# A transformer block on one core: the five engines' calls written in a new order, without the batch loop, and with fewer unread products

## The chip, the cores and the metric

The kernel runs on one core of one Trainium2 chip. The metric is the device time of one execution in microseconds. The core's engines, by the names of the profile, are PE (TensorE, the matrix unit; its weight loads are PEld), DVE (VectorE), ACT (ScalarE), POOL (GpSimd) and SP (SyncE), which issues most of the DMAs.

## The reference, cut to what matters

The input is 8 batches of 512 rows and 256 columns. Each batch goes through one transformer block with a causal window of 128, and then through a gated feed-forward that looks at the row before.

```python
def _L0_attn_ref(x, Wq, bq, Wk, bk, Wv, bv, Wo, bo, W1, b1, W2, b2, ln1_w, ln1_b, ln2_w, ln2_b):
    B, L, D = x.shape                      # 8, 512, 256; 16 heads of 16
    band = (j > i) | (i - j > WINDOW)      # WINDOW = 128
    h = layer_norm(x, ln1_w, ln1_b)
    q = (h @ Wq + bq).reshape(B, L, N_HEADS, HEAD_DIM)   # k and v likewise
    scores = jnp.einsum('blhd,bmhd->bhlm', q, k) * scale + bias
    attn = jax.nn.softmax(scores, axis=-1)
    ctx = jnp.einsum('bhlm,bmhd->blhd', attn, v).reshape(B, L, D)
    x = x + ctx @ Wo + bo
    h2 = layer_norm(x, ln2_w, ln2_b)
    return x + jax.nn.gelu(h2 @ W1 + b1) @ W2 + b2       # W1: 256 x 1024

mod = (_silu(c) @ wmod).reshape(B, 6, 1, -1)   # sa, ca, ga, sb, cb, gb
h = _layernorm(x) * (1 + ca) + sa
x = x + ga * _L0_attn_ref(h, ...)
h = _layernorm(x) * (1 + cb) + sb
r = sigmoid((mu_r * h + (1 - mu_r) * h_prev) @ W_r.T)    # h_prev: the row before
k = (mu_k * h + (1 - mu_k) * h_prev) @ W_k.T
x = x + gb * (r * (square(relu(k)) @ W_v.T))
```

## The kernel before

The work is cut into 8 batches; u counts the 16 half-batches of attention (eight heads each) and i the 16 half-batches of rows in the feed-forward parts; gp counts the 64 groups of four heads. Every engine has its own instruction stream, written by hand as a list of calls such as `project(3)` or `scores(7, 2, 4)`. A call waits on semaphores for its inputs and for its buffers, issues its instructions, and raises a semaphore. So the order on an engine is exactly the order of its list, and an engine stands still when the call whose turn it is lacks an input, whatever is ready behind it.

One half-batch of attention goes through these calls. `transposes_a` (PE), `high_a` (ACT) and `low_a` (DVE) turn the normalised rows and split them into a high and a low half precision part. `project` (PE, 12 products) makes queries and keys, `high_qk` (ACT) and `low_qk` (DVE) split them. `maxima(u, 0..3)` on PE makes upper bounds of the scores and the call of the same name on DVE reduces them (tile nmax); the four of one u take turns on PE and DVE. `max_rows` (PE), `max_copy` (ACT), `low_m` (DVE) and `max_send` (ACT) put the maxima beside the queries. `stacks` (SP) brings queries and keys into the layout of `scores` (PE, two pieces per group: `(gp, 0, 2)` and `(gp, 2, 4)`); `exps` (ACT) takes the exponential of each piece, `select` (POOL) cuts the band, `sums` (POOL) adds for the denominators, and `context(u)` (PE) multiplies with the values, which `values` (PE) and `copy_v` (ACT) have made. `copy_den` (ACT), `fold_den`, `save_den`, `spread_den` (SP), `divide` and `scale_c` (DVE) finish the softmax. `out_project` (PE) and `residual_a` (DVE) end attention.

The first feed-forward of a half-batch i is `stats_b` (DVE), `rstd_b` (POOL), `norm_b` (ACT), `transposes_b` (PE), `high_b` (ACT), `low_b` (DVE), `up` (PE), `gelu` and `high_f` (ACT), `low_f` (DVE), `down` (PE). The second is `residual_b` (DVE), `rstd_c` (POOL), `norm_c` (ACT), `transposes_d` (PE), `modulate` (ACT), `mix` (DVE), `keys`, `receptance` and `values_b` (PE), `square` and `gate` (ACT), `gated` (DVE), `scale_o` (POOL), `output` (DVE) and `store` (SP).

All this is a pipeline over the batches. The first part of the lists (the fill) is written out and starts the batches one after the other; PE, ACT, DVE, POOL and SP then have a loop (`for b in range(3, 7)` on PE and ACT) whose body holds one batch's worth of each kind of work; the last part empties the pipeline. Between the calls of the fill PE has `warm(n, times)`: products of an identity matrix with itself whose result is never read (line 239, each shows in the trace as two matmul records). Up to the end of the fill there are 146 of them, and 16 more in `warm_end(0, 16)` (line 244) before the last `keys`. Setup work (rounding and splitting of weights, `setup_w1`, `setup_wo`, `setup_w2` on ACT; squares, gates and norms, `setup_gates` and `setup_f1` on POOL) stands in the fill too.

The lines of the trace: 239 `warm`, 244 `warm_end`, 267 to 269 `project`, 285 to 287 `values`, 303 and 307 `maxima`, 342 `scores`, 361 to 381 `context`, 398 `out_project`, 430 to 432 `up`, 486, 474 and 498 `keys`, `receptance` and `values_b` on PE; 958 to 964 `high_qk`, 976 `copy_v`, 983 `copy_den`, 997 `exps`, 1146 `setup_w1` on ACT; 1530 `maxima`, 1562 `residual_a`, 1667 `output`, 1623 `mix` on DVE; 2104 to 2112 `setup_gates`, 2174 to 2179 `select` on POOL.

## Time and profile before

| what | value |
|---|---|
| time, median of 3 runs | 622.04 us (620.81 to 622.77) |
| time of the profiled execution | not listed apart from its span; the fastest of the 3 runs is 620.81 us |
| its span in the trace | 620.5 us |
| PE busy | 567.8 us, 92% |
| ACT busy | 446.9 us, 72% |
| DVE busy | 403.2 us, 65% |
| POOL busy | 380.3 us, 61% |

The span is the time from the first to the last instruction in the trace. Busy time of PE counts the unread products as well. PE is the engine with the most work in every stretch, but its share is an average over the fill, the loop and the end, which have different limits.

### The profile page before, as it was taken

How to read it: one execution, taken by the hardware profiler on the slowest of the kernel's cores; microseconds unless marked ns; L12 is line 12 of the kernel's file. 1: busy time of each engine (PE TensorE's matmuls, PEld its weight loads, DVE VectorE, ACT ScalarE, POOL GpSimd, SP SyncE). 2: the span in 40 equal slices, each digit the busy share in tenths (PEclk: the TensorE clock that was granted, in tenths of full speed). 3: DMA queues.
4: the chain of work that ended last, by engine and by line, in shares of the span. 5: the costliest groups of instructions: out<-in, count | busy, mean ns of one | idle time of the engine just before them, and what ended most of it. 6: DMA issues, size and time to landing. Idle time of an engine off the chain costs nothing.

```text
span 620.5 us, 16499 instructions
## 1 busy us (share of the span) xinstructions
PE 567.8 (92%) x6528; PEld 444.8 (72%) x6528; DVE 403.2 (65%) x830; ACT 446.9 (72%) x745; POOL 380.3 (61%) x610
## 2 busy tenths in 40 slices
PE   5889988999898999999898989899999989999996
PEld 2668757777776777677667767677767768878785
DVE  4676746686464788576867686578867475375453
ACT  2527447499968777897879786987788798955542
POOL 4387324657937957675767678586657378943430
PEclk9989989899999999999999999999999999999999
DMA  5635423434503051351235132533134242110111
GB/s 176 246 103 133 124 77 78 112 75 116 137 18 101 25 139 52 97 143 56 69 90 153 60 87 76 146 93 89 52 80 112 70 116 52 54 46 26 34 44 35
DMA packets 46364, 55.74 MB, mean 90 GB/s; under 512 B 11643, under 2 KB 33469, under 8 KB 46286
## 3 DMA queue, kind: packets, MB, share of 16 engines
q1 hardware_dynamic: 44454, 53.81, 31.4%
q8 instruction: 52, 0.85, 0.6%
q10 hardware_dynamic: 1832, 0.87, 0.6%
q14 instruction: 26, 0.21, 0.1%
HBM read 22.31 MB, written 4.49 MB: 43 GB/s over the span
## 4 chain that ended last, share of the span: by engine, by line
PE 50%; ACT 17%; DVE 15%; issue 7%; POOL 7%; DMA 1%; SPq 1%; ACTq 1%; DVEq 0%; POOLq 0%
PE rest L486 4%; PE rest L498 4%; PE rest L447 3%; PE rest L449 3%; PE rest L448 3%; DVE nmax L1530 3%; PE quad L342 3%; ACT rest L1048 3%; PE rest L361 3%; PE rest L474 3%; PE rest L239 3%; PE quad L398 2%; ACT hid_hi L1058 2%; ACT p L997 2%; DVE hid_lo L1590 2%
## 5 line engine op out<-in xcount | busy, mean ns | idle before, releaser
L2174 POOL TENSOR_SCALAR_AFFINE_SELECT p<-p 128x448 f32<-128x448 f32 x64 | 41.5, 649 | 102.8 <-ACT p L997 80.5
L1530 DVE TENSOR_REDUCE nmax<-quad 128x8 f32<-128x1032 f32 x64 | 79.0, 1234 | 2.2
L430 PE MATMUL rest<-bt_hi,w_hi 128*128 128x256 f16 x256 | 70.2, 274 | 5.3 <-DVE hid_lo L1590 5.1
L997 ACT ACTIVATE p<-quad,scale_s 128x576 f32<-128x576 f32 (+1 forms) x77 | 62.3, 822 | 15.7 <-PE quad L342 15.4
L1048 ACT ACTIVATE rest<-rest,bias,scale_g 128x256 f32<-128x256 f32 x128 | 63.0, 532 | 11.2 <-PE rest L432 11.0
L447 PE MATMUL rest<-w_hi,hid_hi 128*128 128x256 f16 x256 | 69.9, 273 | 0.9 <-DVE hid_lo L1590 0.9
L432 PE MATMUL rest<-bt_hi,w_lo 128*128 128x256 f16 x256 | 69.8, 273 | 0.0
L431 PE MATMUL rest<-bt_lo,w_hi 128*128 128x256 f16 x256 | 69.8, 273 | 0.0
L449 PE MATMUL rest<-w_hi,hid_lo 128*128 128x256 f16 x256 | 69.8, 272 | 0.0
L448 PE MATMUL rest<-w_lo,hid_hi 128*128 128x256 f16 x256 | 69.8, 272 | 0.0
L1590 DVE SCALAR_TENSOR_TENSOR hid_lo<-rest,inv_f,hid_hi 128x512 f16<-128x512 f32 x64 | 46.8, 744 | 25.1 <-ACT hid_hi L1058 24.8
L2189 POOL TENSOR_TENSOR ps<-p 128x384 f32<-128x384 f32 x56 | 56.7, 1012 | 1.4
L2191 POOL TENSOR_TENSOR ps<-ps,p 128x320 f32<-128x320 f32 x56 | 49.1, 877 | 4.4
L342 PE MATMUL quad<-q_st,k_st 100*128 100x192 f16 (+3 forms) x468 | 45.1, 228 | 6.8 <-DVE x L1562 2.7
L1058 ACT ACTIVATE hid_hi<-rest,inv_f 128x512 f16<-128x512 f32 x64 | 43.4, 687 | 4.5 <-PE rest L449 2.2
L342 PEld LDWEIGHTS quad<-q_st,k_st 100*128 100x128 f16 x468 | 33.1, 97 | 16.7 <-issue 3.7
L1527 DVE COPY_PREDICATED quad<-later,quad 128x248 f32<-128x248 int16 x64 | 26.8, 418 | 28.2 <-PE quad L307 28.1
L361 PE MATMUL rest<-p,v_blk 128*32 128x192 f32 (+2 forms) x1024 | 41.2, 314 | 0.9 <-POOL p L2179 0.9
L361 PEld LDWEIGHTS rest<-p,v_blk 128*32 128x32 f32 x1024 | 31.9, 112 | 12.8 <-issue 5.8
L239 PE MATMUL rest<-ident 128*128 128x128 f32 x292 | 41.1, 292 | 0.0
L239 PEld LDWEIGHTS rest<-ident 128*128 128x128 f32 x292 | 37.1, 202 | 1.8 <-issue 0.7
L1517 DVE SCALAR_TENSOR_TENSOR k_two<-kc,pick,k_two 128x512 f16<-128x512 f32 x32 | 24.7, 827 | 20.1 <-ACT kc L964 20.1
(239 smaller groups left out, 1531.9 us busy)
## 6 DMA issues: line engine op xcount, KB each, us to landing
k_st<-k_two SPq DMA_DIRECT2D x64, 128.0 KB, 2.5
v_blk<-vn SPq DMA_DIRECT2D x16, 512.0 KB, 6.4
q_st<-q_two SPq DMA_DIRECT2D x64, 64.0 KB, 2.6
k_st<-k_two SPq DMA_DIRECT2D x64, 64.0 KB, 2.0
rb<-den_rows SPq DMA_DIRECT2D x16, 256.0 KB
x<-x SPq DMA_DIRECT2D x16, 256.0 KB, 3.0
out<-x SPq DMA_DIRECT2D x16, 256.0 KB, 2.2
xa<-x SPq DMA_DIRECT2D x7, 512.0 KB, 4.8
```

The costliest lines, as they stand in the source:

```text
L239: e.matmul(psum[4 if n < WARM else 7 if n < WARM + 5 else 5][:, 0:P], ident[:, :], ident[:, :], start=True, stop=True)
L342: last = e.matmul(bank[:, c0:c0 + w], k_st[0:MR, half, j, s * P:(s + 1) * P], q_st[0:MR, half, j, s * KW + q0:s * KW + q0 + w], start=True ...
L361: e.matmul(bank[32 * j:32 * j + 32, s * KW:s * KW + w], v_blk[:, s % 2, s // 2, half, 2 * j * HD:2 * (j + 1) * HD], p32[(4 * u + j) % SLOT ...
L430: e.matmul(dst, w1_hi[:, k, ms], bt_hi[:, k, :], start=(k == 0), stop=False)
L431: e.matmul(dst, w1_hi[:, k, ms], bt_lo[:, k, :], start=False, stop=False)
L432: last = e.matmul(dst, w1_lo[:, k, ms], bt_hi[:, k, :], start=False, stop=(k == KC - 1))
L447: e.matmul(dst, hid_hi[:, m, ts], w2_hi[:, m, :], start=(m == 0), stop=False)
L448: e.matmul(dst, hid_hi[:, m, ts], w2_lo[:, m, :], start=False, stop=False)
L449: last = e.matmul(dst, hid_lo[:, m, ts], w2_hi[:, m, :], start=False, stop=(m == MF - 1))
L997: e.activation(p32[gp % SLOTS][:, c0:c0 + 2 * w].rearrange("p (n c) -> p n c", n=2), (rest if gp < APART else quad)[:, b0 % HQ:b0 % HQ + 2 ...
L1048: e.activation(dst, dst, ACT.Gelu_apprx_tanh, bias=bias_1[:, m:m + 1], scale=scale_g[:, 0:1]).then_inc(s_gl, 1)
L1530: e.tensor_reduce(nmax[:, :, :, qt].rearrange("p a j -> p j a"), quad[:, :, 2 * QB - 2:2 * WIN].rearrange("p j (c a) -> p j a c", a=2), AX ...
```

## The change

The lists of all five engines are written in another order, and the loop over batches is written out, so that the order can differ from batch to batch. The calls themselves are the same ones, and each does what it did. Of the 146 unread products before the end 82 are left, in other places; the 16 of `warm_end` now stand behind the last `values_b`. A few waits are added, with which statistics and a load don't overwrite what is still to be read. `hold(e, s, n)` is the kernel's own helper, a wait that is left out where an earlier one implies it.

PE, from the start of its lists to the first batches of the fill, then the place of `values_b(0)`, the head of the loop, and the end:

```diff
+            warm(0, 2)
             setup_first()
             setup_mod()
             setup_attn()
             setup_peak()
             setup_row()
-            warm(0, 9)
+            warm(1, 5)
             transposes_a(0)
-            warm(1, 3)
+            warm(2, 14)
             project(0)
-            warm(2, 10)
             warm(3, 3)
+            warm(4, 2)
             maxima(0, 0)
+            warm(5, 11)
             maxima(0, 1)
-            warm(4, 4)
-            warm(5, 1)
-            warm(6, 1)
             maxima(0, 2)
-            warm(7, 6)
+            setup_mod_rest()
             maxima(0, 3)
-            setup_mod_rest()
             max_rows(0)
             values(0, 0)
+            project(1)
+            setup_mod_cols(0, 0)
             values(0, 1)
-            project(1)
             scores(0, 0, 2)
-            warm(8, 10)
+            setup_mod_cols(0, 1)
+            warm(9, 3)
             maxima(1, 0)
-            setup_mod_cols(0, 0)
-            warm(9, 3)
-            warm(10, 3)
             scores(0, 2, 4)
-            setup_mod_cols(0, 1)
+            setup_mod_cols(1, 0)
+            setup_mod_cols(1, 1)
+            scores(1, 0, 2)
             maxima(1, 1)
-            warm(11, 3)
-            scores(1, 0, 2)
-            warm(12, 3)
-            warm(13, 1)
+            warm(11, 2)
+            warm(12, 2)
+            warm(14, 5)
             maxima(1, 2)
             scores(1, 2, 4)
-            warm(14, 6)
             scores(2, 0, 2)
             maxima(1, 3)
-            warm(15, 4)
-            setup_mod_cols(1, 0)
-            setup_mod_cols(1, 1)
+            warm(15, 5)
+            setup_f1()
             scores(2, 2, 4)
             transposes_a(1)
+            setup_bias(0)
             scores(3, 0, 2)
+            setup_bias(1)
             max_rows(1)
-            warm(16, 1)
             scores(3, 2, 4)
             project(2)
-            values(1, 0)
-            warm(17, 5)
             scores(4, 0, 2)
-            warm(18, 1)
-            maxima(2, 0)
-            setup_f1()
-            warm(19, 12)
-            scores(4, 2, 4)
-            maxima(2, 1)
-            setup_bias(0)
-            setup_bias(1)
-            scores(5, 0, 2)
             setup_bias(2)
             setup_bias(3)
+            values(1, 0)
+            setup_bias(4)
+            scores(4, 2, 4)
+            maxima(2, 0)
+            setup_bias(5)
+            scores(5, 0, 2)
+            setup_bias(6)
+            setup_bias(7)
+            maxima(2, 1)
+            warm(18, 1)
+            warm(19, 1)
+            scores(5, 2, 4)
             maxima(2, 2)
-            scores(5, 2, 4)
             context(0)
             scores(6, 0, 2)
+            scores(6, 2, 4)
             maxima(2, 3)
-            scores(6, 2, 4)
-            setup_bias(4)
-            setup_bias(5)
-            setup_bias(6)
+            scores(7, 0, 2)
+            scores(7, 2, 4)
             max_rows(2)
-            scores(7, 0, 2)
             project(3)
             values(1, 1)
-            scores(7, 2, 4)
-            setup_bias(7)
             scores(8, 0, 2)
             context(1)
             setup_f2()
+            maxima(3, 0)
             scores(8, 2, 4)
-            maxima(3, 0)
             scores(9, 0, 2)
-            warm(20, 3)
             transposes_a(2)
             scores(9, 2, 4)
-            warm(21, 3)
-            warm(22, 3)
             maxima(3, 1)
+            warm(20, 4)
             scores(10, 0, 2)
+            maxima(3, 2)
             scores(10, 2, 4)
-            maxima(3, 2)
-            warm(23, 3)
             scores(11, 0, 2)
             maxima(3, 3)
+            warm(22, 1)
+            warm(23, 6)
             scores(11, 2, 4)
-            warm(24, 3)
-            warm(25, 2)
-            out_project(0)
             max_rows(3)
             project(4)
-            out_project(1)
+            out_project(0)
             context(2)
             scores(12, 0, 2)
+            out_project(1)
+            scores(12, 2, 4)
             transposes_b(0)
-            warm(26, 1)
-            scores(12, 2, 4)
-            warm(27, 3)
-            warm(28, 4)
-            warm(29, 1)
             maxima(4, 0)
+            warm(25, 0)
             up(0, 0, 1)
-            warm(30, 3)
             maxima(4, 1)
             up(0, 1, 2)
-            warm(31, 1)
-            warm(32, 2)
             maxima(4, 2)
             up(0, 2, 3)
             maxima(4, 3)
-            warm(33, 7)
+            warm(26, 5)
+            warm(27, 2)
             scores(13, 0, 2)
             values(2, 0)
             scores(13, 2, 4)
-            warm(34, 5)
             scores(14, 0, 2)
             scores(14, 2, 4)
-            transposes_b(1)
             max_rows(4)
             scores(15, 0, 2)
             values(2, 1)
             scores(15, 2, 4)
+            transposes_b(1)
             up(0, 3, 4)
             project(5)
             scores(16, 0, 2)
             context(3)
-            warm(35, 6)
+            warm(30, 5)
             maxima(5, 0)
-            warm(36, 7)
+            warm(31, 1)
+            warm(34, 1)
+            warm(35, 1)
+            up(1, 0, 1)
             scores(16, 2, 4)
             scores(17, 0, 2)
-            up(1, 0, 1)
             scores(17, 2, 4)
             up(1, 1, 2)
...
             scores(21, 2, 4)
+            values_b(0)
             scores(22, 0, 2)
             scores(22, 2, 4)
...
-            for b in range(3, 7):
-                u = 2 * b
-                gp = 8 * b
-                scores(gp - 1, 0, 2)
-                values(b, 1)
-                down(u - 4, 0)
-                maxima(u, 3)
-                keys(u - 5)
...
+            scores(23, 0, 2)
+            values(3, 1)
+            down(2, 0)
+            maxima(6, 3)
+            keys(1)
+            transposes_b(3)
+            scores(23, 2, 4)
...
+            keys(15)
+            receptance(15)
+            values_b(15)
             warm_end(0, 16)
-            keys(NU - 1)
-            receptance(NU - 1)
-            values_b(NU - 1)
```

ACT:

```diff
             setup_silu()
+            load_ones()
             setup_attn()
             norm_a(0)
             setup_wqk()
             high_a(0)
-            high_qk(0)
             setup_sq1()
             setup_wv()
-            load_ones()
+            high_qk(0)
+            copy_v(0, 0)
             max_copy(0)
             max_send(0)
-            copy_v(0, 0)
+            high_qk(1)
             copy_v(0, 1)
-            high_qk(1)
             exps(0, 0, 2)
             exps(0, 2, 4)
+            exps(1, 0, 2)
+            norm_a(1)
+            exps(1, 2, 4)
             setup_sq2()
-            exps(1, 0, 2)
-            exps(1, 2, 4)
-            norm_a(1)
             exps(2, 0, 2)
             exps(2, 2, 4)
             high_a(1)
             exps(3, 0, 2)
             max_copy(1)
+            max_send(1)
             exps(3, 2, 4)
-            max_send(1)
             high_qk(2)
+            exps(4, 0, 2)
             copy_v(1, 0)
-            exps(4, 0, 2)
             exps(4, 2, 4)
             exps(5, 0, 2)
             exps(5, 2, 4)
+            setup_w1()
+            setup_wo()
             copy_den(0)
             exps(6, 0, 2)
             exps(6, 2, 4)
+            exps(7, 0, 2)
             max_copy(2)
-            setup_w1()
             max_send(2)
-            exps(7, 0, 2)
             exps(7, 2, 4)
             high_qk(3)
+            exps(8, 0, 2)
             norm_a(2)
             copy_v(1, 1)
-            exps(8, 0, 2)
             copy_den(1)
             exps(8, 2, 4)
-            setup_wo()
             exps(9, 0, 2)
```

DVE, an added wait and three places of its list:

```diff
+                hold(e, s_xve, n)
+                if n == 2:
+                    e.wait_ge(s_hn, NT)
                 stats(xa, st_x, mv_x, range(NT), s_xst, s_xmv, 4 * n)
...
+            setup_pick()
             stats_x(0)
-            setup_pick()
             setup_first()
             scale_x(0)
             shift_x(0)
+            stats_h(0)
             setup_mod()
             setup_attn()
-            stats_h(0)
...
+            maxima(3, 3)
             scale_c(1)
-            maxima(3, 3)
+            low_m(3)
+            stats_x(3)
             residual_a(0)
-            stats_x(3)
             stats_b(0)
-            low_m(3)
+            low_qk(4)
             residual_a(1)
-            scale_x(3)
-            low_qk(4)
+            stats_b(1)
...
-            output(NU - 2)
-            mix(NU - 1)
...
+            mix(15)
+            output(14)
```

POOL:

```diff
+            setup_ones()
             rstd_x(0)
-            setup_ones()
             rstd_h(0)
             setup_inv()
             rstd_x(1)
             modulate_x()
+            rstd_h(1)
+            select(0)
+            bias_h(0)
+            select(1)
             setup_gates()
-            select(0)
-            rstd_h(1)
-            select(1)
-            bias_h(0)
             select(2)
+            rstd_x(2)
             select(3)
-            rstd_x(2)
+            setup_f1()
             select(4)
             select(5)
-            setup_f1()
+            rstd_h(2)
             select(6)
             select(7)
-            rstd_h(2)
             select(8)
+            bias_h(1)
+            sums(8)
             select(9)
-            sums(8)
+            sums(9)
             select(10)
-            sums(9)
+            setup_f2()
```

SP:

```diff
+            rows_mod()
             load_x(1)
             rows_bias()
-            rows_mod()
+            load_mod_a(1)
             load_w2()
-            load_mod_a(1)
             stacks(0, 0, 2)
+            stacks(0, 2, 4)
+            load_mod_a(2)
             load_v(0)
-            stacks(0, 2, 4)
-            rows_gates()
```

Three places of the order follow, as instructions. The first is PE at the second half of the scores of group 4, in the fill. Here `L342` is scores, `L303` and `L307` are maxima, `L239` the unread products, `L574` `setup_f1`, `L566` `setup_bias`, and `L286`, `L287` the end of `values`. Before:

```order
L574 MATMUL rest<-fro,ones 128x2
L239 MATMUL rest<-ident 128x128 x12
L342 MATMUL rest<-q_st,k_st 128x192
L342 MATMUL rest<-q_st,k_st 128x96 x2
L342 MATMUL rest<-q_st,k_st 128x128
L342 MATMUL rest<-q_st,k_st 128x64
L307 MATMUL quad<-k_two_0,q_two_0 32x320 x16
L566 MATMUL rest<-col,stage_1 128x1 x4
L342 MATMUL rest<-q_st,k_st 128x192 x4
```

and after the change:

```order
L286 MATMUL quad<-wa_lo,at_hi 128x256
L287 MATMUL quad<-wa_hi,at_lo 128x256
L566 MATMUL rest<-col,stage_1 128x1 x2
L342 MATMUL rest<-q_st,k_st 128x192
L342 MATMUL rest<-q_st,k_st 128x96 x2
L342 MATMUL rest<-q_st,k_st 128x128
L342 MATMUL rest<-q_st,k_st 128x64
L303 MATMUL quad<-k_two_0,q_two_0 32x256 x4
L303 MATMUL quad<-k_two_0,q_two_0 32x192 x4
L303 MATMUL quad<-k_two_0,q_two_0 32x128 x4
L303 MATMUL quad<-k_two_0,q_two_0 32x64 x4
L307 MATMUL quad<-k_two_0,q_two_0 32x64 x4
```

The second piece of group 4 (128x192 down to 128x64) had twelve unread products and a `maxima` ahead of it; now `values` and one `setup_bias` stand there, and the `maxima` comes behind it.

The second place is ACT around `copy_den(0)` (tile dn): p32 are the exponentials of groups 5 to 7, m_t and the DMA are `max_copy(2)` and `max_send(2)`, w1_hi is `setup_w1`, wo `setup_wo`. Before:

```order
L997 ACTIVATE p32_5<-rest,scale_s 128x576
L983 ACTIVATE dn<-quad 128x512
L997 ACTIVATE p32_6<-rest,scale_s 128x768
L997 ACTIVATE p32_6<-rest,scale_s 128x576
L938 ACTIVATE m_t<-quad 32x128
L1146 ACTIVATE w1_hi<-stage_1,col_1 128x1024 x2
L945 DMA q_st<-m_t 4x16x128
L997 ACTIVATE p32_7<-rest,scale_s 128x768
L997 ACTIVATE p32_7<-rest,scale_s 128x576
```

and after the change:

```order
L1150 ACTIVATE p32_5<-rest,scale_s 128x576
L1299 ACTIVATE w1_hi<-stage_1,col_1 128x1024 x2
L1273 ACTIVATE wo<-wo,scale_s 128x512
L1136 ACTIVATE dn<-quad 128x512
L1150 ACTIVATE p32_6<-rest,scale_s 128x768
L1150 ACTIVATE p32_6<-rest,scale_s 128x576
L1150 ACTIVATE p32_7<-rest,scale_s 128x768
L1091 ACTIVATE m_t<-quad 32x128
L1098 DMA q_st<-m_t 4x16x128
L1150 ACTIVATE p32_7<-rest,scale_s 128x576
```

The two rows of w1_hi moved from between the exponentials of groups 6 and 7 to ahead of dn, and the weight wo, which stood behind the exponentials of group 8, moved there with them.

The third place is POOL at the first groups: p32_0 to p32_2 are cut by `select`, x2 and mod_g or mod_o belong to `setup_gates`, nb_h, ve_h and rs_h to `rstd_h(1)`. Before:

```order
L2112 TENSOR_TENSOR x2<-x2,mod_o 8x256
L2174 AFFINE_SELECT p32_0<-p32_0 128x7x64
L2177 AFFINE_SELECT p32_0<-p32_0 128x64
L2179 AFFINE_SELECT p32_0<-p32_0 128x6x64
L2137 TENSOR_SCALAR nb_h<-mv_h 128x4
L2138 TENSOR_SCALAR ve_h<-mv_h 128x4
L2140 TENSOR_TENSOR rs_h<-ve_h,mhalf 128x4
L2142 TENSOR_TENSOR nb_h<-nb_h,rs_h 128x4
L2174 AFFINE_SELECT p32_1<-p32_1 128x7x64
L2177 AFFINE_SELECT p32_1<-p32_1 128x64
L2179 AFFINE_SELECT p32_1<-p32_1 128x6x64
```

and after the change:

```order
L2587 AFFINE_SELECT p32_0<-p32_0 128x7x64
L2590 AFFINE_SELECT p32_0<-p32_0 128x64
L2592 AFFINE_SELECT p32_0<-p32_0 128x6x64
L2615 TENSOR_TENSOR h0<-h0,row_b 128x512
L2587 AFFINE_SELECT p32_1<-p32_1 128x7x64
L2590 AFFINE_SELECT p32_1<-p32_1 128x64
L2592 AFFINE_SELECT p32_1<-p32_1 128x6x64
L2516 TENSOR_SCALAR mod_g<-x2 8x256
L2518 TENSOR_SCALAR mod_g<-mod_g 8x256
L2520 TENSOR_TENSOR x2<-x2,mod_g 8x256
```

`setup_gates` ended ahead of `select(0)`, with `rstd_h(1)` behind both; now it begins behind `select(1)`, and `rstd_h(1)` stands ahead of `select(0)`.

## Rows read from the trace of the kernel before

**Rows 1.** The page: span and busy time of each engine

```profile
span 620.5 us, 16499 instructions
PE 567.8 (92%) x6528; PEld 444.8 (72%) x6528; DVE 403.2 (65%) x830; ACT 446.9 (72%) x745; POOL 380.3 (61%) x610
```

**Rows 2.** Windows by stage: length, PE, PEld, DVE, ACT, POOL, PE clock, DMA share, GB/s

```profile
0.00:46.00 46.00, 34.86 (x270) 23.45 (x271) 28.80 (x86) 16.35 (x31) 24.59 (x38) 0.96 0.53 174
46.00:110.00 64.00, 57.08 (x850) 45.77 (x849) 39.94 (x81) 38.92 (x59) 29.73 (x55) 0.94 0.42 109
110.00:154.00 44.00, 42.10 (x558) 33.30 (x556) 31.81 (x66) 34.41 (x56) 28.11 (x46) 0.97 0.36 90
154.00:206.00 52.00, 47.28 (x544) 37.50 (x545) 30.92 (x62) 41.44 (x68) 36.05 (x56) 1.00 0.31 83
206.00:473.00 267.00, 250.10 (x3011) 191.90 (x3009) 191.89 (x385) 218.76 (x366) 184.61 (x294) 1.00 0.34 91
473.00:620.50 147.50, 136.36 (x1304) 112.87 (x1302) 79.86 (x155) 96.98 (x169) 77.23 (x125) 1.00 0.20 56
```

**Rows 3.** Windows of line 239 alone: length, PE, PEld, PE clock, DMA share, GB/s

```profile
46.00:110.00 64.00, 17.14 (x129) 15.29 (x129) 0.94 0.42 109
110.00:154.00 44.00, 13.08 (x90) 11.64 (x90) 0.97 0.36 90
```

**Rows 4.** Waits of PE: us in total, times, longest us

```profile
PE quad L307 <- DVE nmax L1530: 8.5, 12, 2.4
PE quad L342 <- DVE x L1562: 2.7, 4, 0.7
PE quad L342 <- ACT dn L983: 0.8, 5, 0.2
```

**Rows 5.** Timeline of PE, 61 to 76: start, us, instruction, records

```profile
...
64.47 0.27 PE L285 MATMUL quad<-wa_hi,at_hi 128*128 128x256 f16 x1
...
65.78 1.28 PE L239 MATMUL rest<-ident 128*128 128x128 f32 x10
66.90 0.49 PE L342 MATMUL rest<-q_st,k_st 100*128 100x192 f16 x4
...
68.53 2.92 PE L239 MATMUL rest<-ident 128*128 128x128 f32 x24
71.29 0.42 PE L342 MATMUL rest<-q_st,k_st 100*128 100x192 f16 x5
```

**Rows 6.** Timeline of PE and ACT, 84 to 94

```profile
84.90 0.61 PE L267 MATMUL quad<-at_hi,wa_hi 128*128 128x512 f16 x1
84.94 1.13 ACT L1146 ACTIVATE w_hi<-stage,col 128x1024 f16<-128x1024 f32 x1
...
89.18 0.27 PE L285 MATMUL quad<-wa_hi,at_hi 128*128 128x256 f16 x1
...
90.49 0.42 PE L342 MATMUL rest<-q_st,k_st 100*128 100x192 f16 x5
...
91.58 0.68 ACT L958 ACTIVATE q_two<-quad,bias_q 128x512 f16<-128x512 f32 x1
```

**Rows 7.** Window of project(3), all engines, columns as in rows 2

```profile
84.90:88.30 3.40, 3.40 (x11) 1.19 (x10) 0.28 (x1) 3.00 (x4) 0.52 (x2) 0.50 0.20 64
```

**Rows 8.** Timeline of PE, 108 to 125

```profile
109.91 2.46 PE L239 MATMUL rest<-ident 128*128 128x128 f32 x10
...
114.04 0.38 PE L267 MATMUL quad<-at_hi,wa_hi 128*128 128x512 f16 x1
...
118.45 2.49 PE L361 MATMUL rest<-p,v_blk 128*32 128x192 f32 x64
```

**Rows 9.** Timeline of POOL, 41 to 66

```profile
41.93 1.07 POOL L2104 TENSOR_SCALAR mod_g<-x 8x256 f32<-8x256 f32 x1 [2.32 <-DVE x L1677]
...
51.29 0.71 POOL L2112 TENSOR_TENSOR x<-x,mod_o 8x256 f32<-8x256 f32 x1
...
63.63 0.55 POOL L2179 TENSOR_SCALAR_AFFINE_SELECT p<-p 128x384 f32<-128x384 f32 x1
```

**Rows 10.** Timeline of PE, 190.5 to 204: values_b(0)

```profile
192.56 1.97 PE L498 MATMUL rest<-wb,mixed 128*128 128x256 f32 x8
```

**Rows 11.** Timeline of PE and DVE at the end

```profile
606.84 3.74 PE L244 MATMUL quad<-ident 128*128 128x128 f32 x32
...
608.70 0.69 DVE L1667 TENSOR_TENSOR x<-x,tr 128x512 f32<-128x512 f32 x1
```

1820 lines of the change are left out of this document (1173 added, 647 removed).

## The prediction

> **What bounds the kernel now.** I began with the busy times of the page [rows 1]: PE works 567.8 of 620.5 us, so under 53 us of its span are idle. That alone would leave little to win, but it mixes stages, so the next view was the windows by stage [rows 2]. In the first 46 us PE waits for loads and setup; from 46 to 154 us it is busy 99.2 of 108 us; in the loop (206 to 473) 250.1 of 267. The third view splits off the unread products [rows 3]: they fill 17.14 us of the stretch from 46 to 110 and 13.08 us of the one from 110 to 154. PE's real load there is 39.9 of 64 and 29.0 of 44, about 64%. So the fill is not bound by PE's work. It is bound by the chains through the other engines (the longest total among PE's waits is `maxima` on PE for the reduction on DVE, 8.5 us in 12 waits [rows 4]) and by what happens to stand ahead of a ready call. The loop is bound by PE nearly throughout.
>
> So the questions are where an unread product or a misplaced call delays a chain in the fill, and whether the delay is carried to the end. Once the fill is over PE has few gaps, thus a start of the loop that comes x us earlier is an end x us earlier, so long as the other engines come along.
>
> **The change, part by part.** The steps follow the chain of a half-batch from place to place; each gives how much earlier the place comes than before.
>
> *Up to 68 us.* `project(1)` now stands ahead of `values(0, 1)`. One `values` call takes 1.3 us (from 64.47 to 65.78 for the same call of another batch [rows 5]), so `project(1)`, `high_qk(1)` and the first reduction of u = 1 come 1.3 us earlier. `rstd_h(1)` no longer stands behind `setup_gates` and `select(0)`, and 17 of the 29 unread products between `scores(0, 0, 2)` and `maxima(1, 3)` go. Most of them stood in gaps of the reductions' turns, so I take 0.7 us (ends: 0, and 17 times 0.27 = 4.5, with 0.27 us a product from 17.14 us for 129 records at two a product [rows 3]). Together 2.0 earlier.
>
> *`scores(4, 2, 4)`, at 71.29 now.* Ahead of it stand `warm(17, 5)`, 1.28 us, and `warm(19, 12)`, 2.92 us [rows 5]. In the order after the change none of them does; `values(1, 0)` and three bias calls stand there. Its input is the exponential of the first piece, whose `scores` begins at 66.90 [rows 5] and would begin 2 us earlier. Adding one exponential and the bias calls and `values` on PE I get 66.9: 4.4 earlier. From there groups 5 and `context(0)` follow; `maxima(2, 2)` and DVE give back a little, and I carry 4.0. For `context(0)` POOL must have cut group 3, and here a counter term can bite, since `setup_gates` takes 10.1 us on POOL (from 41.93 to 52.00, the end of its last row at 51.29 plus 0.71 [rows 9]) and moves behind `select(1)`. It would begin near 57 and end near 67; `select(2)` and `select(3)` come behind it with `rstd_x(2)`, so group 3 is cut at 69.5 where it is at 64.2 now (the row at 63.63) [rows 9]. `context(0)` would start at 71.2 at the soonest; I find it at about 72.6 with the pieces of group 5 ahead of it. The cover is some 2 to 3 us, so I cost this move at nothing; gone, it costs what it exceeds.
>
> *`high_qk(3)`, at 91.58 now.* `scores(7, 2, 4)` stands behind `project(3)` and `values(1, 1)`: 84.90 to 90.49, 5.6 us [rows 6]. Its exponential stands on ACT ahead of `high_qk(3)`, which so begins at 91.58, 2.2 us after `project(3)` has ended at about 89.3. After the change `scores(7, 2, 4)` is ahead of both, and `setup_w1` (the row at 84.94 and its like, 2.2 us in two) has moved into the time in which ACT waits for `context(0)`. `project(3)` would begin 2.1 us earlier, at 82.8 (the 4.0 of above less 1.9 for the two pieces of group 7 and their exponentials ahead of it). It runs at half clock now: the granted clock of its window is 0.50 for 3.4 us [rows 7], the lower of the two levels, 1.2 GHz. At the full clock its first half would be there 1.4 us after its start, and `high_qk(3)` would begin at 84.9 behind ACT's exponentials: 6.7 earlier. The next reductions follow by 6.8, as DVE is free there.
>
> *110 to 122.* Ten matmul records of unread products, five products, stand from 109.91 to 112.2 or so, with `out_project(0)` up to 114.04, ahead of `project(4)` [rows 8]. The products are gone there and `project(4)` comes first, and `out_project(0)` after it, which nobody waits for yet. For PE that is 2.5 us; together 9.3, with `context(2)` at about 109 instead of 118.45 [rows 8]. The five took 2.46 us here, while ten records at 65.78 took 1.28 [rows 5]: the clock was at half.
>
> *122 to 175.* Another 25 unread products go, 6.8 us at 0.27. Here `up`, `gelu`, `low_f` and the reductions of u = 4 wait for each other over ACT and DVE, and I count nothing for them. The bounds are 0 and 6.8. I take the lower as the products stand in gaps, and carry 9.3.
>
> *`values_b(0)`.* It takes 1.97 us [rows 10] and stands behind `scores(22)`, of which the exponentials are late anyway; before them it fills the wait. I count 2.0: the loop would begin 11.3 us earlier.
>
> *Loop.* `scores` on PE waits 2.7 us in four waits for `residual_a` on DVE and 0.8 in five for `copy_den` [rows 4]. The new order has `transposes_b` or `transposes_d` in front of these pieces, which fills part of them. The bounds are 0 and 3.5, and I take 1.6. Swaps such as `down` and `receptance` I count as nothing: both are ready, both are full PE work.
>
> *End.* `output(14)` stands ahead of `mix(15)` and takes 0.69 us [rows 11]; swapped, it gives 0.7. The 3.74 us of `warm_end` [rows 11] lie in PE's wait for `mix(15)` now and move behind the last product, where DVE and the store end the kernel; they cost nothing there. What may cost is the clock of the last three groups of products, up to 1.7 us by the window of [rows 7].
>
> The rest (added waits, which are met long before; SP's order; setup calls on DVE) I count as nothing: in these stretches DVE is busy 39.94 of 64 us and 31.81 of 44 [rows 2].
>
> **Sum.** 2.0 + 2.4 − 0.4 (to `context(0)`) + 2.8 (to the reductions of u = 3) + 2.5 + 2.0 + 1.6 + 0.7 = 13.6. The span of 620.5 becomes 606.9. It counts on the full clock in all of the fill. With fewer products on PE, I assume one stretch at half clock somewhere in it, 3.4 us at 0.50, which is 1.7 us: 608.6. The median of the runs shown, 622.04, is 1.5 above the profiled span, so the time is 610.1, rounded 610.
>
> **The clock, and a rule that speaks against the change.** The PE clock is 0.94 and 0.97 on the mean in the two windows of the fill and 1.00 from 154 on [rows 2]: even with the products in it the clock falls there in places, among them where PE is fully busy at 84.90 [rows 7] after a stretch of gaps. Half of 3.4 us, 1.7, is the price of each such stretch. The Trainium skill, page "TensorE: Matmul & The Clock Gate", section "What's actually happening", says that the throttled state is the default and that activity releases it. By that rule products that nobody reads are not waste, and taking 64 of them out of a stretch that is two thirds full would lower the clock more often.
>
> **Rivals.**
> - *The clock takes much back.* The mean clocks of the fill, 0.94 over 64 us and 0.97 over 44 [rows 2], are some 10 us at half clock in all, three stretches like that of [rows 7]. They stay, and three or four more come, at 1.7 us each, 5 to 7 us; I take 5.5. For it: the mean clock is below 1 exactly where PE has gaps [rows 2]. Against: many of the removed products lie right before real work, which takes their place with no gap. Time: 610 + 5.5, 615.5. Chance 0.13.
> - *The change does nothing.* The start of the loop is bound by something the new order does not move, and the shift of the fill is absorbed. For it: the stretch up to 154 has DVE and ACT at 72% and 78% from 110 on [rows 2]. Against: the chain passes through the places above. Time 622. Chance 0.06.
> - *Slower.* The place is POOL's queue. `select` and `sums` carry each half-batch to `context`; POOL is busy 69% in the loop [rows 2] with all of its work in one queue. If a batch's period of 66.75 us (267 us over four) grows by a call of 3.4 us on which the next `context` waits, four periods cost 13.6 us and eat the gain; from that the sign turns. With 5 us a period, the time is 610 + 20, and the 1.6 of the loop that isn't got: about 631. For it: the orders of POOL differ from batch to batch in the new code. Against: PE is busy 94% in the loop and POOL has 30% to spare. Chance 0.09.
>
> **How the numbers follow.** The forecast has the chance 0.72. Its own range is 604 to 616: low with all of the loop's waits gone (1.9 more), no half clock (1.7) and 2.4 of the 3.8 us between my value and the bound of the first step; high with the 2.0 of `values_b`, the 2.0 of the first step and the 1.7 of the end lost. The low end of the whole range goes to the removed products' full time: 64 of 109.5 products (219 records), 17.7 of 30.2 us [rows 3], and `values_b`, 19.7 off 622.0, or 602.5. The high end takes in the rival of the clock up to 619.5. A measurement of this kernel tells 0.3% (1.9 us) from no change: faster 0.85 (the forecast and the rival of the clock), same 0.06, slower 0.09.
>
> **What would show it.** In the changed kernel's trace `scores(4, 2, 4)` should stand at about 67, `context(0)` end at 77.3, `high_qk(3)` begin at 85, `context(2)` at 109, and the loop's first call (`scores(23, 0, 2)`) come 11 us earlier than now; the windows of the loop should be 1.6 us shorter in all; `keys(15)` at the end 0.7 us closer to the `transposes_d` ahead of it. Wrong would be: the mean clock of 46 to 154 us under 0.90 (the first rival); an unchanged start of the loop (the second); `context` waiting for a `select` or for `sums` (the third), at `context(0)` or in every period. Were the gain of the fill above 15 us, the products from 122 to 175 did delay the chains, against my zero.

## The result and the profile after

The changed kernel takes 642.22 us (median of 4, 640.32 to 646.11), the kernel before 622.17 us (4 runs): ratio 1.0324 [1.028, 1.0369]. The prediction had said 610.0 and gave "slower" a chance of 0.09. It was wrong in sign, by 32 us. The time of one kernel follows its clock: of the changed kernel's four executions the one with a mean granted clock of 0.979 took 640.32 us, the one with 0.966 took 646.11 us.

The page of the changed kernel, against [rows 1]:

```profile
span 638.6 us, 16293 instructions
PE 560.7 (88%) x6400; PEld 434.6 (68%) x6400; DVE 417.6 (65%) x830; ACT 446.8 (70%) x748; POOL 389.2 (61%) x610
```

PE works 7.1 us less than before and yet the span is 18.1 us longer, so PE idles 25.2 us more. And DVE, with the same 830 instructions, is busy 14.4 us longer: the first sign of something I had not priced. Its windows by stage, columns as in [rows 2], and those of line 239 as in [rows 3]:

```profile
46.00:110.00 64.00, 49.85 (x751) 36.93 (x748) 38.92 (x79) 38.55 (x60) 33.94 (x55) 0.89 0.41 102
110.00:154.00 44.00, 39.95 (x535) 29.71 (x536) 29.43 (x63) 33.70 (x54) 32.19 (x48) 0.93 0.31 76
206.00:473.00 267.00, 239.35 (x2901) 185.77 (x2900) 195.06 (x377) 206.31 (x349) 180.55 (x282) 1.00 0.32 86
46.00:110.00 64.00, 7.62 (x46) 6.49 (x46) 0.89 0.41 102
```

The clock fell from 0.94 to 0.89 and from 0.97 to 0.93: at half clock the fill spends 2 x (0.11 x 64 + 0.07 x 44) = 20 us where it was 10. In the 267 us of the loop PE works 10.8 us less than before.

The places named in the prediction, by the start of each call in the two traces (on PE, where nothing else is said; an empty field means that the prediction gave no value):

| call | before | after | difference | predicted |
|---|---|---|---|---|
| project(1) | 42.98 | 41.18 | −1.80 | −1.3 |
| scores(0, 0, 2) | 45.57 | 46.88 | +1.31 | |
| scores(4, 0, 2) | 66.90 | 65.64 | −1.26 | −2.0 |
| scores(4, 2, 4) | 71.29 | 68.49 | −2.80 | −4.4 |
| context(0), end | 81.34 | 80.92 | −0.42 | −4.0 |
| scores(7, 2, 4) | 90.49 | 85.27 | −5.22 | |
| project(3) | 84.90 | 85.94 | +1.04 | −2.1 |
| high_qk(3), on ACT | 91.58 | 88.69 | −2.89 | −6.7 |
| maxima(3, 1) | 104.58 | 104.94 | +0.36 | −6.8 |
| scores(11, 2, 4) | 109.44 | 114.56 | +5.12 | |
| context(2) | 118.45 | 119.92 | +1.47 | −9.3 |
| scores(23, 0, 2), head of the loop | 206.00 | 206.26 | +0.26 | −11.3 |
| context(6) | 250.71 | 253.00 | +2.29 | |
| up(5, 3, 4) | 300.00 | 305.16 | +5.16 | |
| keys(6) | 379.77 | 389.86 | +10.09 | |
| up(8, 0, 1) | 392.32 | 404.21 | +11.89 | |
| keys(9) | 478.43 | 492.57 | +14.14 | |
| keys(15) | 610.41 | 626.69 | +16.28 | −13.6 |

So there are two separate failures. The fill gained nothing of the 11.3 us. Then the loop and the emptying of the pipeline, on which I had counted −1.6 and −0.7, lost 16 us, in steps of some 1 to 3 us at single calls. The last 1.8 us come behind keys(15).

**Where the fill lost.** PE from 98 to 116, the rows of `scores`, `maxima` and the unread products:

```profile
100.58 0.42 PE L342 MATMUL rest<-q_st,k_st 100*128 100x192 f16 x5
...
104.94 0.36 PE L307 MATMUL quad<-k_two,q_two 32*32 32x320 f16 x16 [3.94 <-DVE at_lo L1825]
105.22 1.83 PE L239 MATMUL rest<-ident 128*128 128x128 f32 x8
...
111.42 3.35 PE L239 MATMUL rest<-ident 128*128 128x128 f32 x14
114.56 0.69 PE L342 MATMUL rest<-q_st,k_st 100*128 100x192 f16 x5
```

`maxima(3, 1)` waits 3.94 us for at_lo, the output of `low_a(2)` on DVE. Then 14 records of unread products take 3.35 us instead of 7 x 0.27 = 1.9, and scores(11, 2, 4), which they hold up, runs at 0.69 instead of 0.42: the granted clock is at its half. In the kernel before, scores(11, 2, 4) started 1.59 us after scores(11, 0, 2), with no product between them. By that distance it could have started at about 111.9 here, an estimate, so the seven products hold it up by some 2.7 us. DVE at that wait, and the piece of the chain that ended last which lies under it:

```profile
103.39 0.35 DVE L1865 RECIPROCAL rc<-rc 128x32 f32<-128x32 f32 x1 [3.86 <-DMA rc<-dn]
103.66 1.22 DVE L1825 TENSOR_TENSOR at_lo<-quad,at_hi 128x512 f16<-128x512 f32 x2
```

```profile
97.73 5.63 DMA rc<-dn
```

`divide(1)` (line 1865) stands ahead of `low_a(2)` on DVE and waits for `fold_den(1)` (rc<-dn), which SP issues behind `load_v(1)`. The transfer takes 5.63 us from its issue. In the kernel before, `divide(1)` stands ahead of `low_a(2)` as well, but SP issues `fold_den(1)` ahead of `load_v(1)`, and the trace shows no wait at `divide(1)`.

**Where the loop lost.** The same pattern, on the same queues. DVE and PE near 304, and SP ahead of it:

```profile
303.76 0.69 DVE L1872 TENSOR_TENSOR ct<-rest,rb 128x512 f32<-128x512 f32 x1 [2.67 <-DMA rb<-den_rows]
304.36 0.74 DVE L1913 SCALAR_TENSOR_TENSOR hid_lo<-rest,inv_f,hid_hi 128x512 f16<-128x512 f32 x1
...
305.16 0.28 PE L430 MATMUL rest<-bt_hi,w_hi 128*128 128x256 f16 x1 [2.54 <-DVE hid_lo L1913]
```

```profile
294.76 1.24 SPq L3007 DMA_DIRECT2D v_blk<-vn  x2
296.10 1.87 SPq L3027 DMA_DIRECT2D rb<-den_rows  x1
```

In the kernel before, SP issued rb<-den_rows ahead of `load_v`:

```profile
291.31 0.61 SPq L2549 DMA_DIRECT2D rb<-den_rows  x1
292.02 1.25 SPq L2529 DMA_DIRECT2D v_blk<-vn  x2
```

`scale_c(7)` on DVE waits 2.67 us for that transfer, `low_f(5, 1, 2)` stands behind it, and `up(5, 3, 4)` on PE waits 2.54 us for `low_f`. Each engine's queue hands the delay on. The other steps of the table read the same way: `up(8, 0, 1)` waits 1.71 us for `low_b(8)`, which `stats_x(7)` now precedes on DVE; `maxima(11, 2)` waits 2.36 us for DVE, whose `residual_b(6)` is late because `bias_h(10)`, `bias_h(11)` and sums precede `rstd_c` and `scale_y(6)` on POOL; `context(6)` waits 0.79 us for `select(27)`, behind `scale_y(3)`.

**DVE's 14.4 us.** The rows of `mix` among the groups of DVE, before and after:

```profile
L1623 DVE SCALAR_TENSOR_TENSOR mixed<-mixed,col,h 128x256 f32<-128x256 f32 x64 | 28.0, 500 | 7.5 <-POOL mixed L2236 7.5
```

```profile
L1947 DVE SCALAR_TENSOR_TENSOR mixed<-mixed,col,h 128x256 f32<-128x256 f32 x64 | 35.7, 618 | 5.2 <-POOL mixed L2649 5.1
```

The same 64 instructions take 7.7 us more. Most of the other 6.7 us are in two more kinds of instruction: the 28 of `scale_x` (like `mix`, with two inputs in SBUF) take 4.1 us more, the 16 of `residual_b` 2.2. The worst is `mix(9)`, DVE and then POOL beneath it (before, its four took 1.66 us):

```profile
485.35 3.80 DVE L1947 SCALAR_TENSOR_TENSOR mixed<-mixed,col,h 128x256 f32<-128x256 f32 x4
```

```profile
485.81 0.93 POOL L2604 TENSOR_TENSOR ps<-ps,p 128x320 f32<-128x320 f32 x1
486.70 1.17 POOL L2602 TENSOR_TENSOR ps<-p 128x384 f32<-128x384 f32 x1
487.95 0.93 POOL L2604 TENSOR_TENSOR ps<-ps,p 128x320 f32<-128x320 f32 x1
```

`sums` (lines 2602, 2604) stands beside `mix` now. keys(4) and keys(6) wait 1.66 and 1.26 us for such a `mix` before they start; in the kernel before, all of PE's waits of this kind come to 1.0 us.

**The end**, PE:

```profile
626.69 2.77 PE L486 MATMUL rest<-mixed,wb 128*128 128x256 f32 x8 [2.75 <-DVE mixed L1947]
629.25 2.85 PE L474 MATMUL rest<-wb,mixed 128*128 128x256 f32 x8
631.94 1.89 PE L498 MATMUL rest<-wb,mixed 128*128 128x256 f32 x8
```

Without `warm_end` ahead of it, PE idles 2.75 us and the next two calls take 2.77 and 2.85 instead of 1.89 each: 1.8 us.

### The profile page after: what moved, and what is told of

Read it like the earlier page. It is cut to its first block, busy times and chain, and to the rows that moved or that the text cites. A ratio compares the mean times of both kernels' runs of the same rounds, so it can differ in the third digit from the quotient of the medians.

```text
span 638.6 us, 16293 instructions
## 1 busy us (share of the span) xinstructions
PE 560.7 (88%) x6400; PEld 434.6 (68%) x6400; DVE 417.6 (65%) x830; ACT 446.8 (70%) x748; POOL 389.2 (61%) x610
## 4 chain that ended last, share of the span: by engine, by line
PE 39%; DVE 21%; POOL 11%; ACT 11%; DMA 8%; issue 8%; SPq 2%; ACTq 0%; POOLq 0%; DVEq 0%
DVE nmax L1852 4%; PE rest L361 4%; DVE mixed L1947 3%; PE quad L398 3%; DMA rb<-den_rows 2%; PE rest L498 2%; PE rest L239 2%; PE rest L474 2%; ACT p L1150 2%; PE rest L447 2%; PE quad L342 2%; PE rest L486 2%; DVE hid_lo L1913 2%; PE rest L449 2%; PE rest L448 2%
## 5 line engine op out<-in xcount | busy, mean ns | idle before, releaser
L1150 ACT ACTIVATE p<-quad,scale_s 128x576 f32<-128x576 f32 (+1 forms) x74 | 60.1, 826 | 17.7 <-PE quad L342 17.4
L342 PE MATMUL quad<-q_st,k_st 100*128 100x192 f16 (+3 forms) x468 | 45.2, 228 | 7.8 <-ACT p L1150 2.5
L342 PEld LDWEIGHTS quad<-q_st,k_st 100*128 100x128 f16 x468 | 33.2, 97 | 17.6 <-issue 3.2
L361 PEld LDWEIGHTS rest<-p,v_blk 128*32 128x32 f32 x1024 | 34.0, 113 | 12.4 <-issue 6.9
L486 PE MATMUL rest<-mixed,wb 128*128 128x256 f32 x128 | 32.4, 397 | 9.1 <-DVE mixed L1947 6.8
L1947 DVE SCALAR_TENSOR_TENSOR mixed<-mixed,col,h 128x256 f32<-128x256 f32 x64 | 35.7, 618 | 5.2 <-POOL mixed L2649 5.1
L307 PE MATMUL quad<-k_two,q_two 32*32 32x320 f16 (+4 forms) x1024 | 22.4, 295 | 18.6 <-DVE nmax L1852 8.4
```

What stands on the lines that cost most here:

```text
L342: last = e.matmul(bank[:, c0:c0 + w], k_st[0:MR, half, j, s * P:(s + 1) * P], q_st[0:MR, half, j, s * KW + q0:s * KW + q0 + w], start=True ...
L361: e.matmul(bank[32 * j:32 * j + 32, s * KW:s * KW + w], v_blk[:, s % 2, s // 2, half, 2 * j * HD:2 * (j + 1) * HD], p32[(4 * u + j) % SLOT ...
L1150: e.activation(p32[gp % SLOTS][:, c0:c0 + 2 * w].rearrange("p (n c) -> p n c", n=2), (rest if gp < APART else quad)[:, b0 % HQ:b0 % HQ + 2 ...
```

## Experiments

The diffs are of the lists of calls, in the engine's name. "Shift" is the start of a call in one trace less that in another. A profile holds one execution, and stretches at half clock in the setup (before 46 us) come in some executions of a kernel and not in others; that is 1 to 2 us of spread. The same holds from 46 to 154 us: five traces (the changed kernel, e1, e4, e5 and e6) have the same calls in the fill, and their mean clocks there differ (table behind e11). Each ratio is against runs of the kernel before in the same session, with medians from 621.5 to 623.0 us.

**e1: the fill in the new order, the rest in the old.** Each list is that of the changed kernel up to the named call, and that of the kernel before from there on.

```diff
 # new order up to:  PE project(7)   ACT norm_b(3)   DVE maxima(6, 3)
 #                   POOL bias_h(6)  SP store(0)
-# behind it: the list of the changed kernel
+# behind it: the list of the kernel before
```

> Each engine follows the order of the changed kernel up to about 215 us (PE up to project(7)), and from there the order of the kernel before. Theory A (single misplaced calls in the loop's lists, each of which stalls the full PE once): the fill alone is worth nothing either way, so 621 to 624 us. Theory B (the loss is made in the fill, by the half clock and the missing unread products, and is carried on): 634 us or more. The changed kernel was 642.2.

Measured: 624.79 us, 1.0043 [1.0015, 1.0071]. That is a little above the range of theory A. So 17 to 18 of the 20 us lie in the order of the loop and the end, 2.6 in the fill. In the loop PE is as busy as before (249.78 of 267 us), while the clock of the same fill is 0.80 in this execution where it was 0.89:

```profile
46.00:110.00 64.00, 53.50 (x737) 40.30 (x736) 39.37 (x86) 37.71 (x59) 34.99 (x57) 0.80 0.38 94
206.00:473.00 267.00, 249.78 (x2997) 191.39 (x2994) 192.16 (x391) 217.39 (x366) 182.48 (x291) 1.00 0.32 88
```

**e2: POOL's whole list put back.**

```diff
-# POOL: the list of the changed kernel
+# POOL: the list of the kernel before
```

> The changed kernel with POOL's whole list in the order of the kernel before. Theory A: the moved bias_h and sums no longer stand ahead of scale_y(6), and mix and shift_x on DVE no longer run beside sums, so mix(4), mix(5), mix(6), mix(9) return from 2.7 to 3.8 us to about 1.7 and residual_b(6) stops waiting; 3 to 6 us less than the changed kernel, 636 to 639. Rival (POOL's order costs nothing, the DMA and DVE lists do): 641 to 643.

Measured: 669.75 us, 1.0772 [1.0707, 1.0836], a miss: the lists fit each other, and the old POOL list against the new four is worse than either set (scores(2, 0, 2) alone waits 5.72 us). It says nothing on POOL's part; e5 and e6 replace it.

**e3: `fold_den(1)` ahead of `load_v(1)`.**

```diff
 # SP
-            load_v(1)
             fold_den(1)
             save_den(1)
+            load_v(1)
```

> The changed kernel with one call of SP moved: load_v(1) behind save_den(1) instead of ahead of fold_den(1). Theory A: divide(1) on DVE gets its input 2 us earlier, low_a(2) behind it too, PE's gap of 3.9 us ahead of maxima(3,1) shrinks to under 2, the clock stays up from 105 to 115, scores(11,2,4) comes 4 us earlier, and the whole 2 to 4 us earlier: 638 to 640. Rival (the later parts of the fill wait for something else): scores(11,2,4) earlier, but the time unchanged at 642.

Measured: 641.88 us, 1.0326 [1.029, 1.0363]. The cause was right: maxima(3, 1) starts at 102.45, scores(11, 2, 4) at 109.01, 5.55 us earlier than in the changed kernel, and the clock from 110 to 154 is 1.00. The shift is still −5.27 at the head of the loop. But then the loop loses it, and the total is unchanged. PE at 227.75:

```profile
227.75 0.43 PE L307 MATMUL quad<-k_two,q_two 32*32 32x320 f16 x16 [2.05 <-DVE nmax L1852]
228.59 0.42 PE L431 MATMUL rest<-bt_lo,w_hi 128*128 128x256 f16 x1
```

After a gap of 2.05 us the products of `up` take 0.42 us instead of 0.27: half clock in the loop, where the kernel before has none. It comes again at 302 us (up(5, 3, 4) takes 2.19) and at the end (keys(15) 3.78). Gaps in the loop cost their length and then the clock.

**e4: `warm_end` ahead of keys(15) again.**

```diff
 # PE
+            warm_end(0, 16)
             keys(15)
             receptance(15)
             values_b(15)
-            warm_end(0, 16)
```

> The changed kernel with the 16 unread products of warm_end ahead of keys(15) again, as before. If the clock's price at the end is real, keys(15) and receptance(15) take 1.9 us each instead of 2.8 and the time is 1.7 to 1.9 us less, 640.4; if those two were slow for another cause, no change (642.2).

Measured: 643.62 us, 1.0352 [1.0318, 1.0386]: nothing to see in the total. In the trace keys(15) and receptance(15) take 1.89 us each again, and values_b(15) comes 1.79 us nearer to keys(15)'s place; against it this execution came to the head of the loop 1.89 us later, and to up(5, 3, 4) 4.00 later, where its calls ran at half clock (2.74 us instead of 1.48). The step of the end is shown in the trace, not in the time.

**e5: POOL's calls put where they don't lie beside `mix`, in the loop only.**

```diff
 # POOL (the moved calls)
+            rstd_b(6), rstd_b(7)   # ahead of sums(34), sums(38)
+            scale_o(4)             # ahead of difference(5)
+            scale_o(5)             # behind rstd_c(6)
+            sums(44), sums(45), sums(52), sums(53)  # each behind its select
```

> The changed kernel with eight calls of POOL moved so that sums and scale_o no longer run beside mix and shift_x on DVE: rstd_b(6) ahead of sums(34); scale_o(4) ahead of difference(5) and rstd_b(7) ahead of sums(38); scale_o(5) right behind rstd_c(6); sums(44), sums(45), sums(52), sums(53) right behind their select. No instruction is added or dropped and no list but POOL's changes. Theory A2 (the two engines get in each other's way on SBUF when both run): mix(4), mix(5), mix(6), mix(9) fall from 2.77, 3.18, 2.67, 3.80 us to under 2.1 each, shift_x(7) from 3.99 to under 2.6, and the time from 642 to about 637. Rival (their long times are waits for data): they keep their length.

Measured: 641.35 us, 1.0289 [1.0249, 1.033]. The duration of `mix` follows POOL: all 64 take 31.0 us instead of 35.7, `mix(4)` 1.66 instead of 2.77, `mix(9)` 2.28 instead of 3.80:

```profile
L1947 DVE SCALAR_TENSOR_TENSOR mixed<-mixed,col,h 128x256 f32<-128x256 f32 x64 | 31.0, 545 | 5.0 <-POOL mixed L2649 4.9
```

That POOL's work stretches it is shown. The total shows no clear gain, but PE's waits do. At keys(4), first the changed kernel, then e5:

```profile
319.18 0.70 PE L486 MATMUL rest<-mixed,wb 128*128 128x256 f32 x2 [1.66 <-DVE mixed L1947]
```

```profile
321.47 0.70 PE L486 MATMUL rest<-mixed,wb 128*128 128x256 f32 x2 [0.55 <-DVE mixed L1947]
```

and within down(10, 0), which waits for a `low_f` behind `mix(9)`:

```profile
490.87 0.28 PE L447 MATMUL rest<-w_hi,hid_hi 128*128 128x256 f16 x1 [1.33 <-DVE hid_lo L1913]
```

```profile
492.39 0.28 PE L447 MATMUL rest<-w_hi,hid_hi 128*128 128x256 f16 x1 [0.23 <-DVE hid_lo L1913]
```

The wait of keys(6) falls from 1.26 to 0.58. Together these three are 2.9 us on PE. Against them stand two stretches at half clock in the loop, near 308 and 383 us, which the changed kernel's trace doesn't have; at each the shift against the changed kernel grows by some 1.7 us. So the shift is +0.89 at the head of the loop, +2.87 at up(8, 0, 1) and +1.55 at keys(11). The contention costs PE some 3 us of the loop, and in this execution the clock takes as much back.

**e6: twelve calls put back to where the trace of the changed kernel shows a wait for them.**

```diff
 # SP: ahead of load_v(4)
+            spread_den(7)
 # SP: ahead of store(2)
+            stacks(8, 0, 2)
+            stacks(8, 2, 4)
 # POOL: bias_h(10), bias_h(11) behind rstd_c(6); scale_y(3) behind sums(27)
 # DVE: stats_x(7) behind maxima(12, 1); shift_x(7) behind maxima(12, 3)
 # DVE: mix(9), output(8) behind low_f(10, 3, 4); scale_c(5) behind low_f(3, 0, 1)
 # DVE: add_y(12) ahead of mix(11)
```

> The changed kernel with single calls of the loop moved to where they stood before, none of them for the contention of e5: SP spread_den(7) ahead of load_v(4) and stacks(8) ahead of store(2); POOL bias_h(10) and bias_h(11) behind rstd_c(6), scale_y(3) behind sums(27); DVE stats_x(7) behind maxima(12,1), shift_x(7) behind maxima(12,3), mix(9) and output(8) behind low_f(10,3,4), scale_c(5) behind low_f(3,0,1), add_y(12) ahead of mix(11). Theory A: PE's gaps ahead of up(5,3,4) (2.5), maxima(11,2) (2.4), up(8,0,1) (1.7), scores(47,2,4) (1.1), down(10,0) (1.5) and transposes_d(12) (1.0) shrink, in sum 7 us: 635. If the gaps come back elsewhere, 640 or more.

Measured: 637.02 us, 1.0227 [1.0168, 1.0285]. That lies between the two expectations (635, and 640 or more). It is the cleanest comparison of the loops: in the two traces the head of the loop comes at the same time to 0.01 us, though at another clock in the fill, and neither loop has half clock. Then the shift against the changed kernel grows to −1.21 at context(6), −2.35 at up(5, 3, 4), −5.10 at up(8, 0, 1) and −6.29 at keys(15). PE works 243.66 of the loop's 267 us instead of 239.35. So some 40% of the loop's loss is due to these calls, each a small move on an engine that I had called two thirds busy. The medians differ by 5.2 us; both profiled executions are the fastest of their kernel. One of the twelve is `mix(9)`, so a part of this is contention as in e5.

**e7: 18 unread products more in the new fill.**

```diff
 # PE
+            warm(6, 6)            # ahead of maxima(0, 2)
+            warm(7, 6)            # ahead of max_rows(0)
+            warm(17, 6)           # ahead of scores(4, 0, 2)
```

> The changed kernel with 18 unread products added in three of PE's gaps of the fill (6 ahead of maxima(0,2), 6 ahead of max_rows(0), 6 ahead of scores(4,0,2)). Theory B (the clock): project(1) at 41 us takes 2.75 instead of 4.2 us and the stretch of 6.8 us at half clock at 71 to 78 is shortened; scores(6,0,2) comes 2 to 4 us earlier, the end 1 to 4 us earlier (638 to 641). If the clock of those stretches does not depend on the products, project(1) stays at 4.2 and the time at 642.

Measured: 643.29 us, 1.0312 [1.0258, 1.0366]: no gain. project(1) takes 2.75 us again instead of 4.20, and project(3) 5.33. Neither can be put down to the products: e6, whose fill is that of the changed kernel, has the same 2.75 and 5.33. The mean clocks of 0.85 and 0.91 lie within the spread of the unchanged fill, so 18 products at these three places show no effect.

**e8: e3 to e7 together.**

> The changed kernel with the moves of e3, e4, e5, e6 and the products of e7 together. If the causes add up: the fill gives 5 us, the loop 10 to 12, the end 1.8, so 642 less 17 to 19: 623 to 625, the kernel before. If the clock falls in the loop again for another gap, 1.7 us more for each.

Measured: 630.76 us, 1.013 [1.0087, 1.0173], 11.5 us better than the changed kernel, still 8 slower than before, and outside the expected 623 to 625. Two stretches at half clock remain in the loop. Against the kernel before, the shift is −2.32 at the head of the loop and +8.71 at keys(15): with all repairs the loop and the emptying still lose 11.0 us.

**e9 and e10: the best fill with the old rest.** e9 is e1 with `load_v(1)` moved as in e3 and with mix(15) ahead of output(14). e10 has in addition:

```diff
 # DVE: setup_f2() ahead of divide(1)
 # PE
-            warm(20, 4)
+            warm(21, 2)
+            warm(20, 6)           # ahead of maxima(3, 1)
+            warm(22, 2)           # ahead of scores(10, 2, 4)
```

> As e1 (fill of the changed kernel, rest in the order before) with load_v(1) behind save_den(1) as in e3, and mix(15) ahead of output(14). If the 5 us that e3 showed at 125 us come through a loop that has no gaps of 2 us, the loop starts 3 to 5 us earlier than before and the time is 617 to 620 against 622; each stretch at half clock more in the fill takes 1.7 off that. If the gain of the fill can't be had, 622 to 625 as e1.

> As e9, with setup_f2 on DVE ahead of divide(1) (so that the bank of these products is free earlier) and 10 unread products between scores(9,2,4) and scores(10,2,4) instead of 4 behind maxima(3,1). If more products in PE's gaps hold the clock, the half clock of 100 to 117 us shrinks to 3.4 us or less and the time is 2 to 5 us under e9; if they only delay, it is e9 or 1 us more.

Measured: e9 622.58 us, 0.9999 [0.9979, 1.0019]; e10 622.63, 1.0002 [0.9978, 1.0026]. e9 is some 2 us better than e1, by the move of `load_v(1)` and the swap at the end; the six products more of e10 show nothing. The gains expected of both did not come. The new order of the fill with 82 products equals the old order with 146. What the order is worth by itself needs a comparison at the same number of products, and e11 gives it.

**e11: the kernel before, with only 64 unread products taken out.** The order is untouched; each `warm(n, ...)` from n = 8 on gets the count that the changed kernel gives it (many 0), so it has 82 like the changed kernel.

```diff
 # PE
-            warm(8, 10)
+            warm(8, 0)
 ...
-            warm(17, 5)
+            warm(17, 0)
 ...
-            warm(36, 7)
+            warm(36, 0)
```

> The kernel before, with the unread products from 46 to 154 us cut from 109 to 45 (each warm(n, ...) from n = 8 on has the number that it has in the changed kernel, 0 where that has none) and nothing moved. Theory B (the clock eats what they free): half clock in the fill grows from 10.2 us to 20 or more, and the time is 622 or up to 4 us more. Rival (they are pure delay in front of ready calls): 3 to 6 us less, 616 to 619.

Measured: 630.03 us, 1.0125 [1.0104, 1.0145]. This separates the clock from the order. With less to do on PE the kernel is some 7.8 us slower (1.25%), more than either expectation allowed. Its windows of the fill:

```profile
46.00:110.00 64.00, 52.89 (x747) 41.60 (x745) 37.90 (x79) 38.34 (x58) 27.65 (x51) 0.83 0.36 93
110.00:154.00 44.00, 38.94 (x456) 28.91 (x458) 30.98 (x63) 30.11 (x49) 27.31 (x47) 0.89 0.41 100
154.00:206.00 52.00, 45.19 (x571) 35.28 (x561) 29.79 (x52) 41.28 (x66) 32.07 (x53) 0.97 0.34 88
```

Half clock: 2 x (0.17 x 64 + 0.11 x 44 + 0.03 x 52) = 35 us instead of 10.

It also shows what the new order of the fill is worth at the same number of products. e11 (old order, 82 products) takes 630.03 us, and e9 (new order, 82 products, `load_v(1)` in its old place) 622.58 in the same session: 7.5 us. (e9 has the swap at the end too, which by e12 and e14 gains nothing.) Without the repair, e1's ratio of 1.0043 against 1.0125 still leaves some 5 us. So the moves did gain, and the removed products cost as much or more.

The mean clock of 46 to 110 and of 110 to 154 us, one trace each:

| fill | unread products | clock, run by run |
|---|---|---|
| old order | 146 | 0.94 and 0.97 (before), 0.95 and 1.00 (e12), 0.97 and 1.00 (e14) |
| old order | 163 | 0.95 and 1.00 (e15), 0.95 and 1.00 (e16) |
| old order | 82 | 0.83 and 0.89 (e11) |
| new order | 82 | 0.89 and 0.93 (changed kernel), 0.80 and 0.90 (e1), 0.87 and 0.91 (e4), 0.81 and 0.92 (e5), 0.81 and 0.93 (e6) |
| new order, 18 more | 100 | 0.85 and 0.91 (e7) |
| new order, `load_v(1)` moved | 82 | 0.89 and 1.00 (e3), 0.89 and 0.92 (e9) |
| the same, more products | 88, 100, 122 | 0.89 and 1.00 (e10), 0.84 and 0.97 (e8), 0.92 and 1.00 (e13) |

**e12 and e14: the new end on the kernel before.**

```diff
 # e12, DVE: mix(15) ahead of output(14); PE: warm_end(0, 16) behind values_b(15)
 # e14, DVE: the same; PE: warm_end(0, 13) stays ahead of keys(15)
```

> The kernel before with two calls moved: warm_end(0,16) behind values_b(15), and mix(15) ahead of output(14). Theory B: keys(15) begins 0.7 us earlier, but keys(15) and receptance(15) take 2.8 instead of 1.9 us each: 1.1 us more, 623. If the clock stays up at the end, 0.7 us less.

> The kernel before with mix(15) ahead of output(14) and warm_end(0,13) instead of (0,16), both still ahead of keys(15). keys(15) begins 0.7 us earlier at full clock: 621.6 against 622.3, hardly to be told from it.

Measured: e12 623.62 us, 1.0023 [1.0003, 1.0043]; e14 623.65, 1.0013 [0.9997, 1.0029]. PE in e12:

```profile
609.80 2.44 PE L486 MATMUL rest<-mixed,wb 128*128 128x256 f32 x8 [2.76 <-DVE mixed L1955]
612.03 3.17 PE L474 MATMUL rest<-wb,mixed 128*128 128x256 f32 x8
```

keys(15) comes 0.61 us earlier, and it and receptance(15) lose 0.55 and 1.28 us to the clock. e14 keeps 13 of the products and still gains nothing that can be measured.

**e13: e10 with 34 products more**, in the gaps of the new fill: those of e7 and

```diff
 # PE
+            warm(4, 4)            # ahead of maxima(0, 0)
+            warm(19, 3)           # ahead of scores(2, 0, 2)
+            warm(19, 5)           # ahead of maxima(2, 2)
+            warm(24, 4)           # ahead of out_project(0)
```

> As e10, with 34 more unread products in PE's gaps of the fill: 4 ahead of maxima(0,0), 6 ahead of maxima(0,2), 6 ahead of max_rows(0), 3 ahead of scores(2,0,2), 6 ahead of scores(4,0,2), 5 ahead of maxima(2,2), 4 ahead of out_project(0). Theory B: the half clock at 41 us and that at 71 to 78 us go or shrink, e10's 17 us of it in the fill fall to 10 or less, and the time is 2 to 4 us under e10 and before: 618 to 621. If half clock stretches only move, 622 to 624.

Measured: 619.92 us (median of 10, 615.84 to 622.22), 0.9954 [0.9934, 0.9974]: faster than both kernels. Its windows:

```profile
46.00:110.00 64.00, 53.35 (x798) 41.62 (x799) 41.17 (x87) 39.14 (x60) 35.16 (x58) 0.92 0.37 91
110.00:154.00 44.00, 39.72 (x554) 29.65 (x552) 30.59 (x65) 34.56 (x55) 31.92 (x49) 1.00 0.36 97
```

With 122 products up to the end of the fill (146 before, 82 in the changed kernel) the clock is about that of before. At like clocks the new order is ahead.

**e15 and e16: is it the products alone?** e15 is the kernel before with 17 more products at five places, e16 that with the end of e14.

```diff
 # PE
+            warm(3, 8)            # ahead of maxima(0, 1)
+            warm(16, 3)           # ahead of scores(3, 2, 4)
+            warm(18, 1)           # ahead of maxima(2, 0)
+            warm(23, 3)           # ahead of scores(10, 2, 4)
+            warm(23, 2)           # ahead of maxima(3, 3)
```

> The kernel before with 17 unread products more in PE's gaps, nothing moved: 8 ahead of maxima(0,1), 3 ahead of scores(3,2,4), 1 ahead of maxima(2,0), 3 ahead of scores(10,2,4), 2 ahead of maxima(3,3). Theory B: the half clock at 33.7 us and at 108.8 us goes (1 to 1.7 us each where PE is busy): 619.5 to 621.5. If the products only delay, 622.5 to 623.5.

> e14 and e15 together: 619 to 621 if both hold; 622 or more if neither does.

Measured: 622.39 us, 0.9988 [0.9969, 1.0007], and 622.10, 0.9992 [0.9978, 1.0005]. The clock is 0.95 and 1.00, and the time stays. That clock can't be put down to the added products: e12 and e14 have 0.95 and 0.97, then 1.00, with the fill of before. The 17 products show no effect, against the expected 619.5 to 621.5. The 0.5% of e13 need the new order of the fill and the products together, and don't come from its end (e14).

## Why the prediction was wrong, by its steps

Two parts of the sum failed. The head of the loop came 11.6 us later than forecast, by the price of the clock (e11) and by one transfer on SP's queue (e3) above all. The loop and the end, whose swaps "I count as nothing", hold the other 20 us.

**"0.7 us" for 17 products, and everywhere that a removed product counted as a gain.** This is the step that failed first. I had the rule that speaks against it, put the clock at "one stretch at half clock somewhere in it ... 1.7 us" in the sum, and at 5.5 us in the rival. e11 measures it: taking out 64 products costs some 7.8 us net in the old order, where I had counted the room of those ahead of scores(4, 2, 4) (4.2 us) and of project(4) (2.46 us) as won. The first rival had this mechanism, with its price too low. Its sign, a mean clock under 0.90 from 46 to 154 us, was just missed in the changed kernel's trace (0.91) and is met in the four others with the same fill. The argument that "many of the removed products lie right before real work, which takes their place with no gap" did not hold where the real work is not ready: PE idles 2.03 us ahead of scores(4, 0, 2) now, where five products stood. The Trainium skill, page "TensorE: Matmul & The Clock Gate", section "What's actually happening", has the throttled state as the default that activity releases. The traces agree: in the old order the clock of 46 to 110 us is 0.94 to 0.97 with 146 products and 0.83 with 82.

**"Together 2.0 earlier", up to 68 us.** project(1) did come 1.80 us earlier, but took 4.20 instead of 2.75 us at half clock, and behind it scores(0, 0, 2) came 1.31 us later. That half clock comes and goes between executions: e1, e5 and e6 have the same fill and 2.75 us. Of the 2.0 at 68 us, 1.26 came (scores(4, 0, 2)).

**"4.4 earlier" and "I carry 4.0".** scores(4, 2, 4) came 2.80 earlier. `context(0)` took 6.72 us, part of it at half clock, and ended 0.42 earlier, against 4.0. My worry, `setup_gates` on POOL, was covered as said: `context(0)` was not held by `select(3)`.

**"project(3) would begin 2.1 us earlier ... at the full clock".** scores(7, 2, 4) did move by 5.22 us. But project(3) now stands behind it and came 1.04 later, and again ran at half clock (4.01 us), so `high_qk(3)` came 2.89 earlier instead of 6.7. I had subtracted only the length of the two pieces, not the wait for their exponentials (0.99 us at one of them).

**"The next reductions follow by 6.8, as DVE is free there".** DVE was idle, but its queue was not free: `divide(1)` at its head waited 3.86 us for a DMA. "SP's order ... I count as nothing" is the same error from the other side. e3 shows this one swap of SP to be worth 5.3 us up to the head of the loop. Busy shares of 39.94 of 64 us say nothing of an in-order queue whose head waits.

**"The products are gone there", 2.5.** This misread the new list. The five products behind scores(11, 2, 4) are gone, but seven now stand right ahead of it, where none stood. They took 3.35 us at half clock, and scores(11, 2, 4) came 5.12 us later. The rest held: with `project(4)` ahead of `out_project(0)` the shift falls from +5.12 to +1.22 at `project(4)`.

**"2.0" for `values_b(0)`.** The shift falls from +1.11 at scores(21, 0, 2) to +0.26 at the head of the loop, so 0.85 came.

**"Once the fill is over ... a start of the loop that comes x us earlier is an end x us earlier".** Held where the loop is the old one and nothing holds it up (e13 has −0.88 at the head of the loop and −0.83 at keys(15)), but not in the changed kernel: e3's 5.27 us shrank to 1.62 by keys(15).

**"1.6" for the loop and "swaps ... I count as nothing".** The loop and the emptying cost 16.0 us. The third rival had the direction, with a chance of 0.09, and the period of the loop did grow by some 3.1 us (from +0.26 at the head to +12.63 at down(10, 0), four periods later). Its mechanism was only a small part: `context` waits 2.1 us in all for `select` and `sums`, against 0.9 before. The rest comes from calls on SP, DVE and POOL that put a waiting instruction ahead of one that PE needs. e6 gives back 6.3 us with twelve calls, and e5 shows some 3 us for POOL's work beside DVE's, a term that the sum didn't have. PE is 94% busy there in the kernel before, so nearly every gap is kept to the end. e1 shows the whole of it to be the order, as the old one beside the same fill has only 0.7 us of it.

**"0.7" at the end and "warm_end ... cost nothing there".** The 0.7 came: the shift falls from +16.94 at keys(14) to +16.28 at keys(15). The products moved away cost 1.8 us, which I had only as a bound of 1.7 in the range. e12 shows both, and a net of +0.2%.

The range's low end is also off by a little: 622.0 less 19.7 is 602.3, not 602.5. It changes nothing here.

Still open: of the loop's 16 us, e6 explains 6.3 and e5 some 3, which overlap at `mix(9)`; e8 with all repairs leaves 8 us against the kernel before, part of it at half clock. Which calls own the rest was not separated. Products between 81 and 98 us of the fill were not tried.

## What to carry to other kernels

In a hand-ordered pipeline the question for a moved call is not how busy its engine is but what stands at the head of that engine's queue at that time and what it waits for; follow each swap of SP and DVE to the next call of the busiest engine, since there it is kept to the end. Products that nobody reads are part of the schedule: where the granted clock is below 1, a removed one is not a gain until the next real work is known to be ready, and taking out 64 of them cost more than 1% here. Judge a new order at the same number of such products: here the two parts of one change had opposite signs in the fill, and the total hid the gain of one. A mean clock from one trace is a sample: the same fill gave 0.80 to 0.89. And the order of one engine can't be judged against lists made for another (e2).

## What the hardware showed that I had not expected

- A gap on PE inside the loop can be followed by the half clock: 2.05 us of idleness at 228 us in e3, then 0.42 us a product instead of 0.27. The changed kernel itself ran its loop at 1.00 with gaps up to 2.5 us, so a gap alone doesn't decide it.
- DVE's instructions with two inputs in SBUF get longer beside POOL's two-input ones: four of `mix` from 1.66 to as much as 3.80 us, while `low_f`, which reads one input from PSUM, stays at 742 ns (744 before). The Trainium skill, page "SBUF — State Buffer", section "🔬 SBUF: two separate sides", calls the port pair that DVE and GpSimd share an exclusive lock, which a DVE operation with two SBUF inputs needs only against a GpSimd operation that reads SBUF. By that rule the trace agrees in direction; e5, where `sums` moved away and `mix(4)` is back at 1.66 us, agrees too.
- The small transfer rc<-dn (16 KB) took 5.63 us from its issue behind the two of `load_v(1)` at 98 us, and 2.28 us at 292 us, where `load_v` is issued behind it. rb<-den_rows (256 KB) took 7.63 us at 296 us behind such a pair.
